# A four-batch transformer chain on one core: six weight loads move from SyncE's queue to ScalarE's, and the hand-written order of the first half changes

## The reference

```python
x = _L0_xattn_ref(x, ctx_1024, ..., ctxb_2048x64, ...)  # norm, attention (8 heads), a recurrence s = silu(s @ A.T) + u_t over 1024 steps, plus a row of ctxb
x = _L1_xattn_ref(x, ctx_1024, ...)                     # norm, attention (16 heads of 64), causal mask, added to x
x = _L2_xattn_ref(x, ctx_1024, ctx_1024, mask, ...)     # attention (16 heads of 16) with a multiplied mask, norm after it
x = _L3_xattn_ref(x, ctx_1024, mask, ...)               # norm, masked attention, then norm, fc1, gelu, fc2
```

## Time and profile before

| | |
|---|---|
| median of 3 runs | 1373.4 us (1373.37 to 1373.52) |
| the profiled execution | 1372.36 us, span 1370.6 us |
| PE busy | 1330.6 us, 97% of the span |
| DVE, ACT, POOL busy | 904.9, 673.8, 557.2 us |
| chain that ended last | PE 86%, DVE 6%, POOL 4%, ACT 2% |

### The profile page before, as it was taken

One profiled execution on the slowest core, in us unless ns is written; L12 is line 12 of the kernel. 1 busy time (PEld: TensorE's weight loads), 2 busy tenths in 40 slices (PEclk: granted clock), 3 DMA queues, 4 the chain that ended last, 5 costly groups with the idle time before them and its releaser, 6 DMA issues.

```text
span 1370.6 us, 22991 instructions
## 1 busy us (share of the span) xinstructions
PE 1330.6 (97%) x8763; PEld 1123.3 (82%) x8763; DVE 904.9 (66%) x2204; ACT 673.8 (49%) x1495; POOL 557.2 (41%) x700
## 2 busy tenths in 40 slices
PE   6999999999999999999999999999999999899999
PEld 5889987787888788878888888779877987688778
DVE  4778872777656766676577566773768467746771
ACT  4667766134554444544445534445344543464453
POOL 4464431107513652364245311572166216621661
PEclk9999999999999999999999999999999999999999
DMA  6154402200000000000000001000000000000000
GB/s 150 36 116 132 132 20 81 65 8 1 1 17 17 1 12 6 17 0 9 1 9 1 25 5 29 0 1 17 16 1 1 20 12 1 1 5 12 1 1 17
DMA packets 48363, 34.10 MB, mean 25 GB/s; under 512 B 22077, under 2 KB 45436, under 8 KB 48252
## 3 DMA queue, kind: packets, MB, share of 16 engines
q1 hardware_dynamic: 46919, 32.44, 8.6%
q10 hardware_dynamic: 1332, 0.17, 0.1%
HBM read 23.26 MB, written 8.39 MB: 23 GB/s over the span
## 4 chain that ended last, share of the span: by engine, by line
PE 86%; DVE 6%; POOL 4%; ACT 2%; issue 1%; DMA 0%; ACTq 0%; SPq 0%; DVEq 0%
PE ps L886 11%; PE ps L876 10%; PE ps L836 10%; PE ps L932 8%; PE ps L855 8%; PE ps L943 8%; PE ps L846 6%; PE ps L896 6%; PE ps L802 5%; PE ps L785 5%; PE ps L1037 2%; PE ps L1050 1%; DVE mx L1351 1%; POOL pr L1607 1%; POOL pr L1621 1%
## 5 line engine op out<-in xcount | busy, mean ns | idle before, releaser
L1582 POOL TENSOR_TENSOR rstd<-mv,halfneg 128x1 f32<-128x1 f32 x192 | 108.1, 565 | 339.1 <-DVE mv L1317 337.5
L1621 POOL TENSOR_TENSOR pr<-mx,pr 128x616 f32<-128x616 f32 x128 | 155.8, 1219 | 216.7 <-DVE mx L1351 215.4
L1163 ACT ACTIVATE pr<-pr 128x616 f32<-128x616 f32 x224 | 159.8, 716 | 148.6 <-POOL pr L1621 78.3
L1167 ACT ACTIVATE pr<-ps 128x512 f32<-128x512 f32 x224 | 132.8, 595 | 161.8 <-PE ps L855 161.6
L886 PEld LDWEIGHTS ps<-vtab,pr 128*128 128x128 f32 (+1 forms) x1280 | 153.3, 192 | 14.6 <-ACT pr L1167 10.1
L886 PE MATMUL ps<-vtab,pr 128*128 128x102 f32 (+1 forms) x1280 | 161.9, 275 | 2.3 <-ACT pr L1167 0.9
L855 PE MATMUL ps<-ident,pr 128*128 128x128 f32 (+1 forms) x1120 | 160.0, 276 | 3.7 <-POOL pr L1607 2.9
L1142 ACT ACTIVATE tt<-ps 128x256 f32<-128x256 f32 x160 | 61.0, 382 | 182.3 <-PE ps L785 182.0
L855 PEld LDWEIGHTS ps<-ident,pr 128*128 128x128 f32 (+1 forms) x1120 | 125.9, 140 | 29.9 <-POOL pr L1607 9.4
L876 PE MATMUL ps<-vwo,pr 128*128 128x256 f32 (+1 forms) x640 | 148.9, 381 | 0.0
L836 PE MATMUL ps<-wk,tt 128*128 128x308 f32 x512 | 144.9, 424 | 0.0
(11 more groups left out here) (200 smaller groups left out, 2364.4 us busy)
## 6 DMA issues: line engine op xcount, KB each, us to landing
out_dram<-xt SPq DMA_DIRECT2D x64, 128.0 KB, 1.7
xt<-in_x_dram SPq DMA_DIRECT2D x32, 128.0 KB, 2.2
xt<-out_dram SPq DMA_DIRECT2D x32, 128.0 KB, 2.0
fc<-in_L_xattn_fc_w_dram SPq DMA_DIRECT2D x2, 1024.0 KB, 6.4
wk<-in_L_xattn_wkv_dram SPq DMA_DIRECT2D x4, 512.0 KB, 4.7
front<-in_L_xattn_wkv_dram SPq DMA_DIRECT2D x4, 512.0 KB, 5.8
wo<-in_L_xattn_wo_dram SPq DMA_DIRECT2D x1, 1024.0 KB, 7.8
kb<-in_L_xattn_wq_dram SPq DMA_DIRECT2D x1, 1024.0 KB, 5.5
```

Source lines behind the costliest of these rows:

```text
L1163: ac(v, v, ACT.Exp, scale=-ATTN[key[0]].scale).then_inc(done["expo"], 1)
L1167: ac(pr[:, run.lane, 0:4 * P], bank(run.lane, 0), ACT.Copy).then_inc(done["pturn_main"], 1)
L1621: p.tensor_tensor(p8, mx[:, run.lane, :].unsqueeze(2).to_broadcast([P, HG, KEYS]), p8, ALU.subtract).then_inc(done["below"], 1)
```

## The change

Six entries of `LATE` are issued by a new step `weights_act` in ACT's stream; `weights_get` keeps the others. To place the new steps, the strings in `TURNS` are other ones up to the start of the second half, for all five engines. PE's list of steps is the same 1522 steps, DVE's 2165 and POOL's 649; ACT has six more (1033) and SP six fewer (169). The first 30 steps of PE, 22 of ACT, 17 of SP and 6 each of DVE and POOL stand as before, and so do the last 1123 of PE, 740 of ACT and 1718 of DVE. No computation changes.

```diff
+LARGE = (18, 19, 23, 30, 31, 32)
...
-    steps = [] if pair else ([("v0_put", p)] + [("weights_get", i) for i in range(LOADS - 1)] + wkv1 + [("masks", "2"), ("weights_get", LOADS - 1)])
+    steps = [] if pair else ([("v0_put", p)] + [("weights_act" if i in LARGE else "weights_get", i) for i in range(LOADS - 1)] + wkv1 + [("masks", "2"), ("weights_get", LOADS - 1)])
...
+            def weights_act(i, run):
+                dst, src, signal = LATE[i]
+                act.dma_start(dst, src).then_inc(signal, 16)
+
...
     "gpsimd": (
-        "i012ii2i303i1011001122033203201310011223302003a0121311a222032303030111122223003003311112202030233113012221302033"
+        "i012iii2303i10010111023223023101013012203203023013a111a223232300130011122220300331311012200203323113012212230033"
```

More of the change, by code:

```diff
@@ L196 @@
                "w2_mm", "wqt_mm", "k_mm", "wk_mm", "vt_mm", "vwo_mm", "v_mm", "scan_mm", "gap_turn", "more_pe"),
-    "scalar": ("item_act", "v0_lay", "turned", "query_bias", "expo", "pturn_main", "u_sb", "gelu", "w2_sb", "wqt_sb", "k1_sb", "vt_sb", "silu", "more_act"),
+    "scalar": ("weights_act", "item_act", "v0_lay", "turned", "query_bias", "expo", "pturn_main", "u_sb", "gelu", "w2_sb", "wqt_sb", "k1_sb", "vt_sb", "silu", "more_act"),
     "vector": ("ctx_stats", "ctx_norm", "item_dve", "stats", "aggr", "norm", "bound", "rowmax", "shift", "rowsum", "den_eps", "recip", "weigh",
@@ L236 @@
     "tensor": (
[L237 to L240, removed]
+        "iiiiii0i0i1iii1iii2i102iii2i0ii0ii1ii01ii03120131001301201321302310213021230103321020310132012312030230120301322"
+        "0012332013013211201321320321302213202013301032130201213210210320213012302310031021032131032012031023023012031230"
+        "23310132132012312312032203132030213013213012013203112301231322032301231301213231232301a230a23aasaaaasaasasasasas"
+        "asasasaasaasaasaasaasaasaasaasasaasasasaasasaasaasaasaasaasasaasaasaasaaaa0aaaaa203102s1231030210123120303012010"
         "2132121020303131312020201011313230202012131030302321201010230232103101201020130231320110132132130103012210210323"
@@ L272 @@
     "scalar": (
[L273 to L281, removed]
@@ L282 @@
-        "2201303102313122233"),
+        "iiiii0iii1021ii2i0i10iii102ii1301302001311302101320132022313032001213103a021031203222010303321201311320a1a321202"
+        "2301323302a001321011032101322203a1020021303301231103a20131022230013233201323102131203221013233120300312013112032"
+        "122313032132323110a230a23saasasaasassaasassaasaasaasaaaasaasaaasaasasaasaasssssssssssssss02013201213030120130212"
+        "0123013123020130121320032110303212010202313102010233121013302103120120130130123102011320301032123002132003231120"
@@ new lines @@
+        "0311023212013001323112010233120131230201213003121032210313232003213032121302023103123021310320121032130002231011"
+        "22303103132120320130103221210310321302032130131202302132100131230203013121203203103212bb1323bbbbbb2332bb2bb323bb"
+        "bb23022031031302102321030312023121023131230203103121203023310102211323020113032120013032131032322012103120231030"
+        "1032120312023112330201301321200321310302121003230121313020023131210320221302133102301230301220132102313123020310"
+        "3121203023101032121003231021313012003212130232012301332102023103013212031023121303202301312102302331010221313202"
@@ L1254, in more_act @@
                     act.sem_inc(more_r, MORE)
-            steps = {"item_act": item_act, "v0_lay": v0_lay, "turned": turned, "query_bias": query_bias, "expo": expo, "pturn_main": pturn_main, "u_sb": u_sb,
+            steps = {"weights_act": weights_act, "item_act": item_act, "v0_lay": v0_lay, "turned": turned, "query_bias": query_bias, "expo": expo, "pturn_main": pturn_main, "u_sb": u_sb,
                      "gelu": gelu, "w2_sb": w2_sb, "wqt_sb": wqt_sb, "k1_sb": k1_sb, "vt_sb": vt_sb, "silu": silu, "more_act": more_act}
```

15 lines of the change are left out of this document (8 added, 7 removed).

## The result

The changed kernel takes 1379.1 us (median of 6 runs, 1377.56 to 1382.14) against 1373.46 us for the kernel before (6 runs, 1372.44 to 1374.95). The ratio is 1.0041, with a 95% interval of 1.0031 to 1.0051. It is 5.6 us slower, where I forecast no change, and it also varies more: its runs lie 4.6 us apart. Five of those six are between 1378.5 and 1382.2 us, and the profiled one is the quickest, so the profile shows only a part of what the median holds.

A forecast was written before the change was run, and what follows sets the result against it. PE, busy for 97% of the span, was taken as the bound. Terms -0.4 - 0.3 + 0.4 + 0.2 = -0.1 us on the profiled 1372.4, plus 1.0 to the median, gave 1373.3 us; range 1369.6 to 1375.9.

The forecast's parts named there:

- Six issues on ACT: Six load issues on ACT, 28% free from 60 to 175 us: mostly covered, +0.2 us, at most +3.1.
- What SP saves: SP issues six DMAs fewer, 3.1 us, but waits anyway; transfers keep nearly the same order: 0.
- Rival (B): ACT becomes what PE waits for, all six issues uncovered: +3.1 us, 1376.5 us; 14 in 100.
- Lane 3's first `query`: Its 0.38 us wait for ACT's `turned` goes, as two more groups stand between: -0.4 us.
- `scores`: PE's waits ahead of `scores`, averaging 0.2 us: three follow a `proj` in place of five, -0.3 us.
- `masks`: POOL's block from 82.55 us starts later; PE's stall moves by four groups and `mix` is late: +0.4 us.
- The third is the start of the kernel, up to 31 us, where the first 30 PE steps are the same in both versions, so nothing is to be had.: Start of the kernel, up to 31 us: same first 30 PE steps in both versions, nothing to gain.
- What would make the prediction wrong: First recurrence step 2 us or more from 209.3 us, or a changed time behind it, held for impossible.

The follow-up runs named there:

- e1_issues: Turns of the kernel before, with only the six loads moved from SP's queue to ACT's: 1373.08 us, ratio 0.9999.
- e13: Changed kernel with lane 1's first `pturn` put back ahead of setup item 20 and `masks` moved to POOL's wait near 195.6 us: 1371.72 us.
- e14: Turns of the kernel before, six loads issued by ACT, `masks` moved to POOL's wait near 195.6 us: 1372.81 us.
- e9: Changed kernel with one PE step moved: lane 1's first `pturn` back in front of setup item 20: 1376.4 us.
- e10: e1_issues with lane 1's first `pturn` and its two copies moved behind setup items 20 and 21: 1379.2 us.
- e17: Changed kernel with `masks` in POOL's wait near 195.6 us and five transposes added on PE at the head of setup item 20: 1372.59 us.
- e7_last: Turns of the kernel before up to about 110 us, those of the changed kernel from there to the recurrence: 1374.03 us.
- e15_three_quiet: e13 with the issue of `fc1` fourteen steps earlier on ACT: 1372.02 us.
- e2_turns: Turns of the changed kernel, with the six loads put back on SP's queue: 1378.92 us, ratio 1.0042.
- e6_middle: Turns of the kernel before, but those of the changed kernel from about 45 to about 110 us: 1386.37 us.
- e12_changed_again: The changed kernel itself run once more, for its spread and a second trace: 1378.68 us.
- e4_fc1: Changed kernel with the issue of `fc1` fourteen steps earlier on ACT: 1381.2 us.
- e16_quiet_only: Changed kernel with `masks` alone moved to POOL's wait near 195.6 us: 1374.2 us.

## Why the prediction was wrong

**What held.** *Six issues on ACT*, +0.2, and the 0 of *What SP saves* were right within the measurement: `e1_issues` has these two alone and takes 1373.08 us against 1373.32. Rival (B) fell. The six issues took 0.37 to 0.40 us each, and no wait of PE on ScalarE is longer than the 0.4 us of before. The rule in "DMA: Bandwidth & Descriptors" of the Trainium skill, section "Issuing engines are not separate DMA queues", agrees as far as shown here: `e1_issues` differs from the kernel before by the queue alone, and the times are the same. *Lane 3's first `query`* came as said: in the changed kernel's trace no wait stands ahead of it (44.54 us). The waits ahead of *`scores`* fell from 5.0 to 4.2 us, more than the 0.3 that I took. Whether either is worth anything in time isn't shown. `e13` has the new order and `e14` that of before, both with `masks` in the quiet place, and their runs at a mean clock of 0.999 are alike, 1370.8 to 1371.6 and 1370.7 to 1371.6 us.

Two steps of the prediction failed, one at `masks` and one at the start.

***`masks`*, +0.4.** The waits were right. I had PE wait 1.3 us at the `turn`, and it waited 1.38; I had the `mix` 0.6 us late, and it waited 0.76 us; PE lost 1.75 us in place of 1.36, which is the +0.4. What I put at nothing is what the clock does behind the stall: at 1.2 GHz for 3.3 us, up to 1.7 us more in an execution that has it. The term measured +2.1 us in that trace. In the medians `e9`, with the start mended, is still 3.3 us above the kernel before, and all of this goes with `masks` in its new place (`e13`). I had no term for the granted clock at all. Its column stood in the rows I read, at 1.00, and I took it for a constant. Why this stall lets the clock fall and that of before did not isn't shown. How little PE worked does not decide it: it was busy for 1.29 of 2.50 us here, and for 1.14 of 2.50 from 89.0 us on in the kernel before, which kept 1.00.

**"The third is the start of the kernel, up to 31 us, where the first 30 PE steps are the same in both versions, so nothing is to be had."** This is the other step that failed. I looked at 30 PE steps that are the same and stopped there. The 31st to 35th differ, and they run at 30 to 35 us, just as PE comes out of a wait at the lower clock (0.50 in the kernel before too, from 28.7 to 32.0). With lane 1's `pturn` moved behind four other groups, up to 20 us at the lower clock follow in some executions. `e9`, `e10` and `e17` show this from three sides: 8 of the changed kernel's 11 runs are above 1378 us, and none of the nine of `e9` is. In the medians the step is worth 2.3 to 2.7 us.

***What SP saves*, on transfers.** Some 1 us of the profiled run came from the late x at 157 us, which I had excluded: I argued that the order of DMAs in time is nearly the same. It was not; `fc1` is issued 12 us later than before and meets a store. But the changed kernel's second trace has none of this loss, and in the medians it is nothing (`e7_last`, `e15_three_quiet`), so it made a wrong step but not the wrong result. My first reading of the two traces, too, gave 1.9 us to the start's turns. `e2_turns`, with the same turns there, has none of it, and `e6_middle`, with the turns of before, has its rise at 17.4 us: it is the moment at which the clock rises, and that goes with the execution.

**The range** ended at 1375.9 because rival (B) was its only case on the slow side. "What would make the prediction wrong", a recurrence step 2 us or more away, is what happened (214.69). That the time behind it can't change held for this pair of traces, but not in general: 12 of the 20 traces take 1.5 us longer there, with a fall of the clock in an order that nobody touched.

**What stays open.** Why an execution falls into the upper group or not is not shown. It may go with the moment of the clock's first rise. Nine traces have lane 1's `pturn` late and nothing in its place. The four whose rise is at 16.6 to 17.8 us have 10 to 20 us at the lower clock from 30 us on; the five with a rise at 14.4 to 16.1 or at 18.1 us have 3.4. With the step as before and a rise at 17.2 to 17.4 us (`e6`, `e9`, `e15`) it is 3.4 us as well. I saw this pattern afterwards, and no run tests it.

The price of `masks` is accounted for in part. In one trace its stall and fall are 1.75 + 1.7 = 3.45 us, and taking both away lowers the median by 4.7 (`e9` to `e13`) and brings the first recurrence step from 212.68 to 208.16 us in the profiled pair, 4.5. About 1 us of this has no cause shown. Against the kernel before, `e9` should by its trace lose the 2.1 us at `masks` and the 1.5 of a fall in the second half, 3.6 us; this is an estimate from one trace, and 3.3 were measured.

## What to carry to other kernels

Before calling a stretch of PE unchanged, look at the granted clock's low places in it and at what PE runs there: a step with little work moved next to one of them can cost more than any wait. A long block on an engine that is rarely waited for belongs where that engine idles for longer than the block, even 100 us away; here that, and one step put back, turned 5.6 us lost into 1.4 won, the latter at the edge of what can be measured. And when one kernel's runs lie several us apart while its rival's lie within one or two, take a second trace before explaining the first.

## What the hardware showed that I had not expected

- A gap of PE may not end with itself. PE was busy for 1.56 of 3.30 us (`e2_turns`, 90.4 us), and the clock behind it was 0.50 for the next 3.3. The Trainium skill ("TensorE: Matmul & The Clock Gate", section "HAM oscillation — how this bites in real kernels") tells of a kernel in which waits for DMAs, some 3 to 5 us each, throw PE back to half clock again and again. The traces agree that a wait can do it, and here two of 1.38 and 0.76 us came before a fall. Not every one does: `e12_changed_again`, `e4_fc1` and `e6_middle` have the same two waits and keep 1.00, and so does the kernel before, which lacks 1.36 us from 88 to 92 us.
- The clock can fall far from any change. Twelve of 20 traces have one fall in the second half, at 1.5 us each.
- A PE that is busy without a gap can stay at the lower clock: 10.20 of 10.20 us at 0.50 (`e12_changed_again`, 38.3 us). "Busy" and even "97% of the span" don't tell of it; the matmuls per us do (44 in 10.2 us against 27 in 3.3).
- Five transposes more on PE made a kernel 1.6 us faster in the median (`e17_filled` against `e16_quiet_only`), because the upper half of its runs was gone.
- The moment of the clock's first rise moves from execution to execution, 14.4 us (`e16_quiet_only`) to 18.1 us (the changed kernel) in these traces. Some half of such a difference is lost: with the rise 3.1 us later, the changed kernel's eight matmuls took 3.72 us in place of 2.29, 1.4 us more.
